# Null keys of an attention layer: their values folded into the output projection, their probabilities shared out by VectorE

## Time and profile before

| | |
|---|---|
| three runs | 965.4, 966.75, 969.77 us (median 966.75) |
| profiled execution | 965.4 us |
| its span | 963.7 us |
| busy: PE, DVE, ACT, POOL | 908.8, 741.4, 589.3, 563.5 us |
| one middle pass | 110.3 us |

### The profile page before, as it was taken

One profiled execution on the slowest core, in us unless ns is written; L12 is line 12 of the kernel. 1 busy time (PEld: TensorE's weight loads), 2 busy tenths in 40 slices (PEclk: granted clock), 3 DMA queues, 4 the chain that ended last, 5 costly groups with the idle time before them and its releaser, 6 DMA issues.

```text
span 963.7 us, 21588 instructions
## 1 busy us (share of the span) xinstructions
PE 908.8 (94%) x8309; PEld 704.5 (73%) x8309; DVE 741.4 (77%) x2334; ACT 589.3 (61%) x1235; POOL 563.5 (58%) x496
## 2 busy tenths in 40 slices
PE   1887899999999999999999999999999999999896
PEld 1565678687886878677786878778786878768755
DVE  6885678878788797888788797887887677865366
ACT  4528673857567572876647573875738674695621
POOL 5425763677545963668636874558644854468522
PEclk9989999999999999999999999999999999999998
DMA  6400000000000000000000000000000000000000
GB/s 160 109 0 3 11 2 2 0 13 2 14 1 13 1 13 2 1 12 1 14 1 1 12 2 13 1 12 2 13 1 1 1 1 13 1 1 12 3 1 12
DMA packets 22088, 11.50 MB, mean 12 GB/s; under 512 B 7648, under 2 KB 21344, under 8 KB 21856
## 3 DMA queue, kind: packets, MB, share of 16 engines
q1 hardware_dynamic: 20128, 9.51, 3.6%
q10 hardware_dynamic: 1856, 0.59, 0.2%
HBM read 8.00 MB, written 2.10 MB: 10 GB/s over the span
## 4 chain that ended last, share of the span: by engine, by line
PE 61%; DVE 16%; POOL 16%; ACT 4%; issue 3%; DMA 0%; POOLq 0%; DVEq 0%; ACTq 0%
POOL rnorm L928 7%; PE bank L1720 5%; PE bank L2045 5%; PE bank L2003 4%; PE bank L1722 4%; PE bank L1721 4%; PE bank L1964 4%; PE bank L1873 4%; PE bank L1727 3%; DVE xn L1369 3%; PE bank L2077 2%; PE bank L2078 2%; PE bank L2001 2%; PE bank L1970 2%; PE bank L2028 2%
## 5 line engine op out<-in xcount | busy, mean ns | idle before, releaser
L923 POOL TENSOR_TENSOR rnorm<-sumsq,minus_half 128x16 f32<-128x16 f32 x32 | 93.8, 2933 | 78.1 <-DVE sumsq L1542 78.1
L1179 ACT ACTIVATE square<-bank,bias_k,rnorm 128x256 f32<-128x256 f32 x128 | 65.7, 570 | 50.5 <-PE bank L1964 50.5
L1964 PE MATMUL bank<-qT,kT 64*128 64x256 f32 x512 | 94.8, 389 | 0.0
L928 POOL TENSOR_TENSOR rnorm<-unit,minus_half 128x32 f32<-128x32 f32 x16 | 86.7, 5439 | 2.6 <-DVE unit L1548 2.6
L1970 PE MATMUL bank<-qT,kT 64*128 64x128 f32 x512 | 84.0, 284 | 3.6 <-ACT unit L1185 2.2
L1970 PEld LDWEIGHTS bank<-qT,kT 64*128 64x128 f32 x512 | 71.0, 186 | 18.5 <-ACT unit L1185 6.2
L936 POOL TENSOR_SCALAR_AFFINE_SELECT square<-square 128x512 f32<-128x512 f32 x64 | 46.8, 732 | 59.3 <-ACT square L1185 59.3
L1109 ACT ACTIVATE xaT_hi<-bank 128x256 fp32r<-128x256 f32 x16 | 5.5, 383 | 106.3 <-PE bank L1881 106.3
L1964 PEld LDWEIGHTS bank<-qT,kT 64*128 64x128 f32 x512 | 68.6, 186 | 0.8
L936 POOL TENSOR_SCALAR_AFFINE_SELECT unit<-unit 128x512 f32<-128x512 f32 x64 | 41.3, 650 | 43.8 <-ACT unit L1185 43.8
L1179 ACT ACTIVATE unit<-bank,bias_k,rnorm 128x256 f32<-128x256 f32 x96 | 51.5, 574 | 18.5 <-PE bank L1964 18.5
(11 more groups left out here) (400 smaller groups left out, 2933.9 us busy)
## 6 DMA issues: line engine op xcount, KB each, us to landing
xin<-in_L_attn_x SPq DMA_DIRECT2D x7, 256.0 KB, 2.8
out<-x SPq DMA_DIRECT2D x7, 256.0 KB, 2.3
square<-in_L_attn_w_kv SPq DMA_DIRECT2D x1, 1024.0 KB, 6.1
w_sw<-in_L_ffn_sw_w SPq DMA_DIRECT2D x3, 256.0 KB, 8.0
unit<-in_L_attn_w_q SPq DMA_DIRECT2D x1, 512.0 KB, 4.3
w_out<-in_L_attn_w_out SPq DMA_DIRECT2D x8, 64.0 KB, 2.1
w_ml<-in_L_ffn_ml_w SPq DMA_DIRECT2D x2, 256.0 KB, 6.4
xin<-in_L_attn_x ACTq DMA_DIRECT2D x1, 256.0 KB, 3.2
```

Source lines behind the costliest of these rows:

```text
L923: pool.tensor_tensor(rnorm[:, 1, t, :], sumsq[:, t % 2, :], minus_half[:], ALU.pow).then_inc(a_root.sem, 1)
L928: pool.tensor_tensor(rnorm[:, 0, ts, :], k_sumsq[:, ts, :], minus_half[:].unsqueeze(1).to_broadcast([P, 2, H]), ALU.pow).then_inc(a_kroot. ...
L1179: last = act.activation(early(pr, j), k0, ACT.Exp, bias=bias_k0[:, h:h + 1], scale=by)
L1964: return mm(bank[s][:, 2 * P * i:2 * P * (i + 1)], kT[rs, p, 2 * P * b:2 * P * b + P], qT[rs, p, 2 * P * b:2 * P * (b + 1)], start=True, s ...
```

## The change

Null values no longer take part in the mix. Since (n0 w0 + n1 w1)/den is linear, w0 and w1 are multiplied by w_out once, in the prologue (`w_nulls`, 128 x 128, eight products in `s_fold4`, zero-padded through `nv_pad`), and `a_out` adds one product of the normalised null probabilities (`null_T`) with w_nulls for each tile. The denominators no longer get null products: VectorE adds n0 + n1 itself. ScalarE writes the null exponentials into a padded layout (`null_p`, 32 columns for each of 4 row groups, two instructions); `a_nT` is four whole transposes; VectorE turns bank 3 block by block (`null_rows`) and sums pairs (`null_sum`); each unit adds the sum to the denominators, and after its multiplication scales its null probabilities in place (`share`); after units 3 and 7 they are turned back to `null_T`. ScalarE's and VectorE's work on `null_pT` goes.

`a_out.0` goes to bank 5 and waits only for units 0 to 3 and for `l_hu`; `l_down`'s and `l_x`'s second half go to bank 6 (5 in the first pass); `f_clock` writes bank 3. All lists are written anew.

```diff
 MIDDLE = {
     "PE": """
...
-l_g.1 l_cT a_scores.1 l_u.0 a_mix.0 a_scores.2 a_mix.1 l_u.1 e_turn1 l_c.0 a_scores.3 l_g.2 a_mix.2 l_c.1 a_scores.4
...
+a_scores.1 a_mix.0 l_cT l_g.1 a_scores.2 a_mix.1 e_turn1 l_u.0 l_g.2 l_c.0 a_scores.3 l_u.1 a_mix.2 l_u.2 l_c.1
...
         def out_bank(g, h):
-            return bank[7 if h else 5 if ending(g) else 3]
+            return bank[7 if h else 5]
+
+        def down_bank(g, h):
+            return bank[(5 if first(g) else 6) if h else 4]
...
-            (nk_rows, nkv[:, 0, :]), *((nv_rows[32 * i:32 * i + 32, :], nkv[:, 1, :]) for i in range(3)),
+            (nk_rows, nkv[:, 0, :]), (nv_rows, nkv[:, 1, :]),
...
+            def null_pads():
+                pool.memset(nv_pad, 0.0).then_inc(pads_zeroed, 1)
+                pool.memset(null_p[:], 0.0).then_inc(pads_zeroed, 1)
...
-                act.activation(null_p[:], null_s[:], ACT.Exp).then_inc(a_nexp.sem, 1)
-
-            def null_cols(g):
-                act.wait_ge(a_nT.sem, a_nT.at(g))
-                act.activation(null_pT, bank[3][0:NR, :], ACT.Copy).then_inc(a_nhi.sem, 1)
+                if first(g):
+                    act.wait_ge(pads_zeroed, 2)
+                for k in range(NULLS):
+                    last = act.activation(null_slots[:, :, :, :, k], null_s[:, :, :, k].rearrange("p t (q i) -> p t q i", i=QW), ACT.Exp)
+                last.then_inc(a_nexp.sem, 1)
...
-            def s_null():
-                dve.wait_ge(nv_rounded, 3)
-                low_rows = slice(2 * H * NULLS, NR)
-                link(V.tensor_tensor(w_nv[low_rows, :], nv_heads[low_rows, :], w_nv[low_rows, :].bitcast(F32), ALU.subtract))
...
+            def a_nrows_(g):
+                dve.wait_ge(a_nT.sem, a_nT.at(g))
+                V.transpose(null_rows[:], bank[3][:]).then_inc(a_nrows.sem, 1)
+                dve.wait_ge(a_nrows.sem, a_nrows.at(g, 1))
+                pairs = null_rows[:].rearrange("p (k r) -> p k r", r=32)[:, :, 0:QW * NULLS].rearrange("p k (q n) -> p k q n", n=NULLS)
+                V.tensor_tensor(null_sum[:], pairs[:, :, :, 0], pairs[:, :, :, 1], ALU.add).then_inc(a_nrows.sem, 1)
...
                 V.transpose(den_rows, bank[7][:, 0:2 * P]).then_inc(s.sem, 1)
+                if c == 0:
+                    dve.wait_ge(a_nrows.sem, a_nrows.at(g))
+                blocks = slice(8 * b, 8 * b + 8)
                 dve.wait_ge(s.sem, s.at(g, 4 * c + 1))
-                V.reciprocal(recip[:], den_rows[:, 0::32]).then_inc(s.sem, 1)
+                V.tensor_tensor(den[:], den_rows[:, 0::32], null_sum[:, blocks, q], ALU.add).then_inc(a_tot.sem, 1)
+                if c:
+                    dve.wait_ge(a_nshare.sem, a_nshare.at(g, c))
+                dve.wait_ge(a_tot.sem, a_tot.at(g, c + 1))
+                V.reciprocal(recip[:], den[:]).then_inc(s.sem, 1)
...
+                share = null_rows[:].rearrange("p (k r) -> p k r", r=32)[:, blocks, NULLS * q:NULLS * q + NULLS]
+                V.tensor_tensor(share, share, recip[:].unsqueeze(2).to_broadcast([P, 2 * QW, NULLS]), ALU.mult).then_inc(a_nshare.sem, 1)
+                if q == U // SEQ - 1:
+                    dve.wait_ge(a_nshare.sem, a_nshare.at(g, c + 1))
+                    V.transpose(null_T[:, half(b)], null_rows[:, half(b)]).then_inc(a_nn.sem, 1)
...
+                pe.wait_ge(nv_made, QW)
+                for c in range(8):
+                    mm(bank[3][:, 3 * P:], nv_pad[:, c, :], w_out[:, c, :], start=(c == 0), stop=(c == 7))
...
-                mm(den, of_head[:, P * q:P * (q + 1)], null_pT[:, half(b)], start=True, stop=False, skip_group_check=True)
-                for f in range(2):
-                    mm(parts[f], w_nv[:, (2 * q + f) * P:(2 * q + f + 1) * P], null_pT[:, half(b)], start=(f == 0), stop=False,
-                       skip_group_check=True)
...
             def a_out_(g, h):
-                if ending(g) and h == 0:
+                if h == 0:
                     pe.wait_ge(a_mix.sem, a_mix.at(g, 4 * (U // 2)))
+                    if not ending(g):
+                        pe.wait_ge(l_hu.sem, l_hu.at(g + 1))
...
-                        last = mm(out_bank(g, h)[:, ts], outT[:, c, ts], w_out[:, c, :], start=(c == 0), stop=(c == 7))
+                        mm(out_bank(g, h)[:, ts], outT[:, c, ts], w_out[:, c, :], start=(c == 0), stop=False)
+                    if t == 2 * h:
+                        pe.wait_ge(a_nn.sem, a_nn.at(g, h + 1))
+                    last = mm(out_bank(g, h)[:, ts], null_T[:, ts], w_nulls[:], start=False, stop=True)
                 last.then_inc(a_out.sem, 1)
...
-                    mm(bank[6][:], w_kv.hi[:, 0:P], w_kv.hi[:, 0:N], start=True, stop=True)
+                    mm(bank[3][:], w_kv.hi[:, 0:P], w_kv.hi[:, 0:N], start=True, stop=True)
```

More of the change, by code:

```diff
@@ L59 @@
     "PE": """
[L60 to L64, removed]
+a_m.0 a_m.1 a_null a_k.0 a_k.1 a_t.0 a_m.2 a_kr.0 a_k.2 a_k.3 a_t.1 a_kr.1 a_kt a_m.3 l_turn2 a_v.0 a_t.2 a_v.1
@@ L65 @@
+a_t.3 l_turn3 a_v.2 a_v.3 l_route l_g.0 a_scores.0 a_nT l_u.0 l_cT l_g.1 l_u.1 a_scores.1 l_g.2 a_mix.0 l_c.0
+a_scores.2 a_mix.1 e_turn1 l_u.2 a_scores.3 l_g.3 a_mix.2 l_c.1 a_scores.4 l_u.3 a_mix.3 l_c.2 a_scores.5 a_mix.4
+l_g.4 a_scores.6 l_u.4 a_mix.5 l_c.3 a_scores.7 a_mix.6 l_down.0 l_down.1 l_down.2 l_down.3 a_mix.7 a_out.0 a_out.1
+l_x.0 l_x.1
 """,
     "DVE": """
-a_ss.0 a_u.0 a_null a_ss.1 a_ss.2 a_u.1 a_u.2 a_kss l_turn2 a_ss.3 l_res a_u.3 l_norm a_nexp l_turn3 l_route l_pick
-l_hg.0 e_stats l_coef l_hu.0 e_apply l_hg.1 l_hu.1 a_nT l_cT l_hg.2 a_mix.0 l_hc.0 l_hu.2 a_mix.1 e_scan l_hg.3
@@ L91 @@
+a_scores.4 l_u.3 l_g.3 a_mix.3 a_scores.5 l_c.2 a_mix.4 l_g.4 a_scores.6 a_mix.5 l_u.4 l_c.3 a_scores.7 l_down.0
+a_mix.6 l_down.1 l_down.2 l_down.3 a_mix.7 a_out.0 a_out.1 l_x.0 l_x.1
 """,
     "DVE": """
-f_stats.0 f_stats.1 f_apply.0 f_apply.1 a_ss.0 a_null f_ce f_route a_u.0 f_ce_apply a_ss.1 f_hid.0 a_u.1 a_ss.2
-f_hid.1 f_pick f_ce2 a_u.2 f_hid.2 a_kss f_ce2_apply a_ss.3 f_hid.3 l_turn2 a_u.3 l_res l_norm a_nexp e_stats
-l_turn3 f_out.0 f_out.1 l_route l_pick l_hg.0 f_out.2 l_coef f_out.3 a_nT f_end_stats e_apply a_mix.0 l_hu.0 l_hg.1
@@ L120 @@
-l_down.1 a_mix.7 l_down.2 l_down.3 a_out.0 a_out.1 l_x.0 l_x.1
+f_clock a_m.0 a_m.1 a_null a_k.0 f_turn.0 a_k.1 f_turn.1 f_ce.0 f_ce.1 f_sw.0 a_kr.0 a_t.0 a_m.2 f_sw.1 f_me.0 a_k.2
+f_sw.2 f_ceT a_k.3 f_relu.0 f_relu.1 f_sw.3 a_kr.1 f_ce2 a_kt a_t.1 a_m.3 a_v.0 f_ml.0 f_ml.1 a_t.2 l_turn2 f_me.1
+f_ce2T f_ml.2 f_ml.3 a_v.1 f_out.0 f_out.1 l_turn3 a_t.3 a_v.2 a_v.3 l_route a_scores.0 f_out.2 f_out.3 l_g.0 a_nT
+a_scores.1 l_g.1 l_cT a_mix.0 a_scores.2 a_mix.1 l_g.2 l_u.0 l_c.0 a_scores.3 l_u.1 a_mix.2 l_c.1 a_scores.4 l_u.2
@@ L121 @@
+l_g.3 a_mix.3 l_c.2 a_scores.5 l_u.3 a_mix.4 l_c.3 a_scores.6 l_g.4 l_u.4 a_mix.5 a_scores.7 a_mix.6 l_down.0
+l_down.1 l_down.2 l_down.3 a_mix.7 a_out.0 a_out.1 l_x.0 l_x.1
 """,
     "DVE": """
-f_stats.0 f_stats.1 a_ss.0 f_apply.0 f_apply.1 a_ss.1 a_null a_u.0 f_hid.0 f_ce f_route f_ce_apply f_hid.1 f_hid.2
-a_u.1 a_ss.2 f_ce2 f_pick a_u.2 a_kss f_ce2_apply f_hid.3 a_ss.3 l_turn2 l_res a_u.3 l_norm a_nexp l_turn3 f_out.0
-l_route l_pick f_out.1 f_out.2 l_coef f_out.3 a_nT l_hg.0 l_cT a_mix.0 l_hu.0 l_hc.0 a_mix.1 l_hg.1 l_hu.1
@@ L140 @@
+l_astats.0 l_dstats.1 l_astats.1 a_o.0 a_o.1
 """,
```

247 lines of the change are left out of this document (118 added, 129 removed).

## The result

The changed kernel takes 971.45 us (median of 10 runs, 970.47 to 972.35), the kernel before 968.89 in the same comparison (10 runs, 965.21 to 969.95): a ratio of 1.0036, interval 1.0021 to 1.005. It became slower by about a third of a per cent, where the prediction said 953 and held 941 to 962. The runs of the kernel before are spread over 5 us and its profiled execution (965.4) is one of the fastest, while the changed kernel's took 970.47, so by the spans (963.7 and 968.8) the loss to explain is 5.1 us where the medians differ by 2.6.

A forecast was written before the change was run, and what follows sets the result against it. TensorE's instruction stream was taken to bound the middle passes; six passes at -1.8 (-10.8), first pass -2.5, last attention pass -0.3 and prologue 0 gave -13.6 from 966.75: 953 us, range 941 to 962.

The forecast's parts named there:

- What VectorE gains: VectorE's added work in a middle pass: 0.34 us a unit plus transposes, +4.0 in all, so 94.6 of about 108 busy.
- Where it meets: Units 0 to 6 of a middle pass: TensorE (32.3 us) and VectorE (31.6) equally loaded, 2.0 us of new waits a pass.
- The 0.3 in the score loop: Score steps of a middle pass can't outpace ScalarE's exponentials of four heads: a new wait of 0.3 us.
- the 0.5 ahead of f_ce: Ahead of f_ce in a middle pass, two ScalarE copies without a product between: a new wait of 0.5 us.
- The prediction's own sign of being wrong: The prediction is wrong if TensorE idles under 1 or over 3 us a pass; it expected 1.5 to 2.5.
- What TensorE loses and gains: TensorE's products per pass: null products -3.60 us, transposes of a_nT -0.47, output projection +0.89, sum -3.18.
- The sum of a middle pass: A middle pass: -3.18 from products, -0.63 for the old wait, +2.0 of new waits, so -1.8 us.
- the four waits: New TensorE waits in a middle pass: e_turn1 0.7, unit 4 0.4, score steps 0.3, ahead of f_ce 0.5; together 2.0 us.
- rival 2: The lists hide the new waits (0.5 us or less a pass): -3.3 a pass, 940 to 946; chance 0.22.
- The other passes: LAST_L's pass -1.8 us, first pass -2.5, last attention pass -0.3, prologue 0 within 2.
- (3): VectorE takes over the mix stretch: waits of 3.2 to 4.5 us a pass, no change, 962 to 971; chance 0.12.
- (4): Slower: TensorE's every unit waits for VectorE's multiplication of the unit before; at 0.8 us each, 977; chance 0.06.

The follow-up runs named there:

- batched kernel: The changed kernel with one sharing-out multiplication per four units instead of four, same output; 958.84 us, ratio 0.9903 against the kernel before.
- before_newmid: The kernel before (null products on TensorE) with the changed banks and the new lists of the first, middle and LAST_L passes; 973.50 us, ratio 1.006.
- one_input: The changed kernel with the addition and the sharing-out each replaced by a reciprocal with one SBUF input; 957.62 us, ratio 0.9894 against the kernel before.

## Why the prediction was wrong

**The step that failed is "What VectorE gains"**, the price of the two small operations. It took 0.24 for the addition and 0.10 for the sharing-out, 0.34 a unit. Undisturbed that is right (0.27 and 0.09 from start to start). But the row behind the 0.24 is a reciprocal, which has one input and took 0.20 in every run, whatever GpSimd did; the row behind the 0.10 (551.34) has two, but lies beside one of GpSimd's powers, which did not hold up such operations. Neither could show the price in place, 0.25 and 0.17 more on average, the 3.4 us above. The prediction put GpSimd at nothing without a reason, and did not weigh the Trainium skill's rule on the shared ports.

**Where it meets.** The walk through the lists named e_turn1 with 0.7 and unit 4, behind e_sum and l_hc.1, with 0.4. Both are there: 1.23 and 1.68. In the batched kernel they are 0.61 and 0.45. At unit 4 the difference can be read off the rows: e_sum's second operation was 0.31 too long (1.00 for 0.69) and the addition 0.98 (1.15 for 0.17); 1.68 - 1.29 = 0.39. So both places held, and the waiting for GpSimd was the missing term. The 0.3 in the score loop did not come, and of the 0.5 ahead of f_ce 0.14 did; 0.56 at l_turn3 and 0.44 at l_down came unforeseen. Sum 4.14 against 2.0, and 1.90 in the batched kernel: that the last is so near 2.0 is partly luck, since l_turn3 and l_down stand in for places that did not wait. The prediction's own sign of being wrong, over 3 us idle a pass, is met by 4.35.

**What TensorE loses and gains.** A unit lost 0.44 us (0.45 predicted); the estimate of 0.33 for three products, from the Trainium skill ("TensorE: Matmul & The Clock Gate", section Back-to-back issue gap), was too low, the trace's whole distance right. The transposes fell from 1.00 to 0.49, the projection grew by 1.00 (0.89 predicted). That makes -3.0 instead of -3.18. But TensorE's busy time in a pass fell by 2.0 only (109.69 to 107.68). The missing 1.0 us has no idle row; before_newmid shows 0.8 of it with the old code and the new lists. The prediction priced the lists by waits alone: its second missing term.

**The sum of a middle pass**: -3.0 from the products, +1.0 from the order, +3.7 of idle time (4.35 - 0.64) are +1.7, as measured; predicted was -1.8. Times five that is 17.5 of the error of 18.5 us. With the two operations freed of GpSimd, one_input takes 957.62, inside the prediction's range. Small slips in its working change nothing: the second transpose of a unit is 0.45 by its rows and not 0.48, the four waits add up to 1.9 and not 2.0, and rival 2's pass would be 107.0 and not 106.5.

**The other passes.** LAST_L's was predicted like a middle pass, -1.8, and gave -2.5: it has no e work, and TensorE waits only 0.67 us. Prologue and first pass together -2.1 (-2.5). The last attention pass and what follows +1.2 (-0.3): the second half of its output waits 1.27 us for the last multiplication, 0.88 before, and TensorE waits there for late sums (0.7), which it did not before; the rest is not placed. VectorE's 94.73 busy in a pass fits the predicted 94.6 by accident, since 3.4 of it is waiting.

**The rivals.** The time, 971.45, is at the upper end of (3), 962 to 971 by 3.2 to 4.5 us of waits a pass, and the waits of 4.14 are in its range. But its reason, VectorE's load, is not what made most of them: in one_input the same number of operations leaves 1.89 us of waits. (4) asked for a wait at every unit; there are two. Six starts less a pass gain 12.6 us against the changed kernel; against the kernel before that is 1.0%, some 10 us of the 13.6 forecast.
